# A fused adaLN attention and grouped feed-forward kernel: the first microseconds and the step places laid out anew, and the group scalars spread by DMA from a scratch row in DRAM

## The reference, cut to what matters

```python
x = x + attn(wkv(x, f, f, w1, u1, cond), Wq, Wk, Wv, Wo)      # B, T, C = 4, 256, 256
x = x + ffn(wkv(x, f, f, w2, u2, cond), ...)

def wkv(r, k, v, w, u, time_emb):
    tf = sigmoid(time_emb.sum(-1))
    decay = exp(-exp(w)) * (0.5 + 0.5 * tf)                   # per batch and channel
    ek = exp(min(k, 30)); ekv = ek * v
    # scan forward and backward over time: a = a * decay + ekv, b = b * decay + ek
    euk = exp(min(u + k, 30))
    num = nf + nb - ekv + euk * v;  den = df + db - ek + euk
    return sigmoid(r) * (num / max(den, 1e-8)) * (0.8 + 0.2 * tf)

def ffn(x):                                                   # G = 8 groups of I = 176 rows
    scores = softmax(x @ gate_w.T)                            # top 8 of E = 64 kept: w_e
    flat = w_e[:, inv_map]; scalar = flat.sum(-1)             # scalar: tokens x G
    soft = softmax(where(flat == 0, -1e9, flat))
    xg = x[:, None] + einsum('ngi,ghi->ngh', soft, mask_up_w)
    a = silu(xg @ gate_proj) * (xg @ up_proj)                 # tokens x G x 176
    return einsum('ng,ngh->nh', scalar, a @ down_proj)
```

## Time and profile before

| | us |
|---|---|
| median of 3 runs | 440.38 |
| the three runs | 440.99, 437.19, 440.38 |
| the profiled execution, its own time | 440.88 |
| its span in the trace | 438.8 |
| PE / DVE / ACT / POOL busy in it | 377.0 / 328.7 / 278.4 / 215.2 |

### The profile page before, as it was taken

The page is one execution under the profiler, slowest core; times in us unless marked ns, Lnnn a source line. Parts: engine busy times, 40 slices in busy tenths (PEclk is TensorE's granted clock), DMA queues, the critical chain, the costliest instruction groups (busy, mean ns, idle before and its releaser), DMA issues.

```text
span 438.8 us, 6479 instructions
## 1 busy us (share of the span) xinstructions
PE 377.0 (86%) x1974; PEld 301.9 (69%) x1974; DVE 328.7 (75%) x786; ACT 278.4 (63%) x675; POOL 215.2 (49%) x236
## 2 busy tenths in 40 slices
PE   0096867799998779988899898999899999999996
PEld 0086645587787568776768786787587887888884
DVE  7999568998898997479998889584666768544433
ACT  5444868699789568776879886777275243544321
POOL 4771520549354844513257202418069566786732
PEclk9998999999999998999999899999999999999999
DMA  6913410111111110200112100003023222233001
GB/s 196 323 33 118 133 40 0 49 49 51 48 49 49 49 48 3 93 3 1 48 34 61 70 0 1 24 15 108 1 73 82 98 74 58 84 95 112 25 0 48
DMA packets 11072, 26.83 MB, mean 61 GB/s; under 512 B 1312, under 2 KB 3872, under 8 KB 11040
## 3 DMA queue, kind: packets, MB, share of 16 engines
q1 hardware_dynamic: 11040, 26.44, 19.0%
HBM read 25.39 MB, written 1.05 MB: 60 GB/s over the span
## 4 chain that ended last, share of the span: by engine, by line
PE 51%; DVE 28%; ACT 11%; issue 5%; POOL 3%; DMA 1%; POOLq 0%; ACTq 0%; DVEq 0%
PE acc L1102 5%; PE acc L1104 5%; PE acc L1103 5%; PE ov L1195 4%; PE tr L1124 4%; DVE PR L1038 3%; DVE B L845 3%; PE sc L1173 3%; DVE F L845 3%; PE proj L1102 3%; PE proj L1104 2%; PE proj L1103 2%; PE tr L1104 2%; PE tr L1102 2%; PE sc L1102 2%
## 5 line engine op out<-in xcount | busy, mean ns | idle before, releaser
L568 POOL TENSOR_TENSOR WL<-stage,WH 128x256 fp32r<-128x256 f32 x146 | 120.0, 851 | 110.8 <-ACT WH L638 110.7
L588 POOL TENSOR_TENSOR PR<-PR,RI 128x512 f32<-128x512 f32 x48 | 53.5, 1129 | 85.5 <-DVE RI L1048 85.5
L1102 PE MATMUL proj<-WH,RH 128*128 128x512 f32 x96 | 42.8, 446 | 37.7 <-DVE RL L896 22.5
L1102 PE MATMUL acc<-OH,WH 128*128 128x256 f32 (+1 forms) x172 | 55.3, 321 | 5.0 <-DVE OL L1060 4.3
L601 ACT ACTIVATE PR<-PR,MX 128x128 f32<-128x128 f32 (+1 forms) x128 | 56.6, 455 | 0.5 <-DVE MX L1038 0.5
L1173 PEld LDWEIGHTS sc<-kT,QT 128*128 128x128 f32 x256 | 40.7, 191 | 19.4 <-issue 14.2
L1104 PE MATMUL acc<-OH,WL 128*128 128x256 f32 (+1 forms) x172 | 53.9, 313 | 0.0
L1103 PE MATMUL acc<-OL,WH 128*128 128x256 f32 (+1 forms) x172 | 53.9, 313 | 0.0
L1173 PE MATMUL sc<-kT,QT 128*128 128x128 f32 (+1 forms) x256 | 47.7, 328 | 3.2 <-DVE MX L1038 3.2
L1102 PEld LDWEIGHTS proj<-WH,RH 128*128 128x128 f32 x96 | 18.6, 194 | 45.1 <-issue 40.7
L1195 PE MATMUL ov<-PTS,V 128*128 128x512 f32 x96 | 46.9, 597 | 1.4 <-DVE OL L1060 1.4
(11 more groups left out here) (166 smaller groups left out, 894.9 us busy)
## 6 DMA issues: line engine op xcount, KB each, us to landing
stage<-in_ffn SPq DMA_DIRECT2D x22, 384.0 KB, 3.1
stage<-in_wq SPq DMA_DIRECT2D x8, 512.0 KB, 3.5
stage<-in_wo SPq DMA_DIRECT2D x8, 512.0 KB, 3.5
PR<-in_tables SPq DMA_DIRECT2D x4, 352.0 KB, 7.4
fT<-in_fT SPq DMA_DIRECT2D x4, 256.0 KB, 4.1
xT<-in_xT SPq DMA_DIRECT2D x4, 256.0 KB, 4.5
stage<-in_wk SPq DMA_DIRECT2D x2, 512.0 KB, 4.8
stage<-in_wv SPq DMA_DIRECT2D x2, 512.0 KB, 3.3
```

Source lines behind the costliest of these rows:

```text
L568: i = pool.tensor_tensor(lo[:, c:c + 256], src[:, c:c + 256], hi[:, c:c + 256].bitcast(F32), ALU.subtract)
L588: pool.tensor_tensor(pr, pr, RI[:, m % 4, hs[0]:hs[0] + nh].rearrange("p (h o) -> p h o", o=1).broadcast_to([P, nh, 512 // nh]), ALU.mult) ...
L1102: mm(o, lh, rh, start=first, stop=False, skip_group_check=True)
```

## The change

It has four parts.

1. **Start.** `cond` and `vecs` are loaded from ACT's queue, not SP's. The table `decay` is gone: ACT makes `DEC` from `half` with `edec` as its scale, and `half_mix` and `qks` are made later, inside the first scan call. `EX` is cleared half by DVE ahead of the first reduction and half by POOL right behind its first memset, where POOL cleared all of it behind the first split. The low part of the first key weights, `WL` of ("split", "K", 0), is made by DVE in one operation of 1024 columns, where POOL made it in four.
2. **Projections.** `project` issues the four products with the high part of the weights first and waits for the low part only before the last two.
3. **Places.** `ORDERS`, `START` and the lists of places are changed: among others K1 (0, 2) and the rest of scan call (1, 1) stand earlier, the scores' maximum (C) stands at the end of a place on DVE and not near the start of the next, the key and value steps of pair 1 stand elsewhere, the "ind" steps are gone.
4. **Group scalars.** `GS`, `IND`, `SCX` and the DVE part of route 8 are gone. Route 8 leaves 8 rows of 512 scalars in `SCR`; SP writes them to DRAM, waits, and reads each row back, repeated over the partitions that belong to its group, into one of three buffers `SBC`. The last operation of GU reads `SBC` in SBUF and not the bank `ov`.

```diff
 START = {
-    "PE": [("split", "K", 0), ("small",), ("split", "Q", 0), ("K1", 0, 0), ("R", 0), ("R", 1), ("R", 2),
-           ("K1", 0, 1), ("R", 3), ("R", 4), ("R", 5), ("K3", 0, 0), ("K3", 0, 1)],
+    "PE": [("split", "K", 0), ("small",), ("split", "Q", 0), ("K1", 0, 0), ("R", 0), ("K1", 0, 1), ("R", 1),
+           ("R", 2), ("R", 3), ("R", 4), ("R", 5), ("K3", 0, 0), ("K3", 0, 1)],
...
-    "PE": ["GA", "GB", "GS", "Y", "last", "split"],
-    "ACT": ["GT", "last", "split", "GH"],
+    "PE": ["GA", "GB", "Y", "last", "split"],
+    "ACT": ["GT", "split", "last", "GH"],
...
-    for half, places in (((0, 1), [4, 4, 4, 5, 5]), ((1, 0), [15, 15, 15, 16, 16]), ((1, 1), [19, 20, 20, 21, 21])):
+    for half, places in (((0, 1), [2, 4, 4, 5, 5]), ((1, 0), [15, 15, 15, 16, 17]), ((1, 1), [17, 18, 18, 19, 19])):
...
+            def spread_scalars(f):
+                p, m = divmod(f, FT)
+                if m == 0:
+                    tok = slice(p * PT_, (p + 1) * PT_)
+                    sp.wait_ge(s["rt_act"], 7 * p + 7)
+                    sp.dma_start(group_scalars[:, tok], SCR[:, tok]).then_inc(s["scalars_out"], 16)
+                    sp.wait_ge(s["scalars_out"], 16 * (p + 1))
+                if f >= NBC:
+                    sp.wait_ge(s["a_ready"], f - NBC + 1)
+                for g, lo, hi in group_rows(m):
+                    sp.dma_start(SBC[lo:hi, f % NBC, :], group_scalars[g, p * PT_:(p + 1) * PT_].partition_broadcast(hi - lo)).then_inc(spread_in[f % NBC], 16)
+
             for n in range(6, len(BLOCKS)):
+                if BLOCKS[n][0:2] == ("split", "F") and BLOCKS[n][2] >= 4:
+                    spread_scalars(BLOCKS[n][2] - 4)
                 load(n)
...
+            act.dma_start(cond[:], ins["cond"]).then_inc(s["cond_in"], 16)
+            act.dma_start(vecs[:], ins["vecs"]).then_inc(s["vecs_in"], 16)
...
-                            i = nc.scalar.activation(DEC[:, TE * ch:TE * ch + T], const[:, 0:T], ACT.Identity, scale=0.0,
-                                                     bias=decay[:, L - 1, ch, b:b + 1])
+                            i = nc.scalar.activation(DEC[:, TE * ch:TE * ch + T], half[:, b:b + 1].broadcast_to([P, T]), ACT.Copy,
+                                                     scale=edec[:, 4 * (L - 1) + ch:4 * (L - 1) + ch + 1])
...
-                wait_split(pe, wst)
+                pe.wait_ge(s["split_hi"], SPLIT_NO[wst] + 1)
...
                 for ch in range(CH):
-                    a = [x[:, p, ch, P * t:P * t + P] for x in (RH, RL)]
-                    w = wblock(wst, 512 * ch, 512 * ch + 512)
-                    i = three(proj[:], a[0], a[1], w[0], w[1], ch == 0, ch == CH - 1)
+                    mm(proj[:], rh[ch], wh[ch], start=ch == 0, stop=False, skip_group_check=True)
+                    mm(proj[:], rl[ch], wh[ch], start=False, stop=False, skip_group_check=True)
+                wait_split(pe, wst)
+                for ch in range(CH):
+                    i = mm(proj[:], rh[ch], wl[ch], start=False, stop=ch == CH - 1, skip_group_check=True)
...
-                    dve.wait_ge(s["scal_full"], f + 1)
+                    dve.wait_ge(spread_in[f % NBC], 16 * spread_count(f))
```

More of the change, by code:

```diff
@@ L27 @@
 BIG = 3.0e38
[L28 removed]
+NSTAGE, NSLOT, NPS, NBC = 3, 6, 4, 3
 KCAP = 30.0
@@ L91 @@
-            ("K2", 0, 0), ("wkv", 1, 1, 6)],
-    "POOL": [("split", "K", 0), ("small",), ("clear",)],
+            ("wkv", 1, 1, 0), ("split", "K", 0), ("wkv", 1, 1, 2), ("wkv", 1, 1, 3), ("wkv", 1, 1, 4), ("K1", 0, 0), ("K1", 0, 1),
+            ("wkv", 1, 1, 5), ("K2", 0, 0), ("wkv", 1, 1, 6)],
+    "POOL": [("split", "K", 0), ("small",)],
 }
 RELEVANT = {
-    "PE": {"R": None, "split": None, "small": None, "ind": None, "K1": None, "V": None, "K3": None, "GA": None, "GB": None,
-           "GS": None, "route": (0, 1, 3, 4, 6, 7, 8)},
@@ L98 @@
[L98 removed]
+    "PE": {"R": None, "split": None, "small": None, "K1": None, "V": None, "K3": None, "GA": None, "GB": None,
+           "route": (0, 1, 3, 4, 6, 7, 8)},
+    "ACT": {"split": None, "small": None, "K1": None, "V": None, "K2": None, "K3": None, "table": None,
             "wkv": (1, 6, 7), "gate": (0, 1), "route": (0, 2, 3, 5, 6, 7, 8)},
     "DVE": {"K1": None, "K2": None, "table": None, "onehot": None, "wkv": (0, 2, 3, 4, 5, 6, 8), "gate": (0, 1),
[L101 removed]
+            "route": (1, 2, 4, 5, 6, 7)},
@@ L153, in make_plan @@
     ahead = []
-    for f, places in enumerate(([36, 37, 38], [45, 45, 45])):
-        for kind, i in zip(("GA", "GB", "GS"), places):
+    for f, places in enumerate(([36, 37, 37], [45, 45, 45])):
+        for kind, i in zip(("GA", "GB"), places):
             if i < END:
@@ L218 @@
 PLAN = PLANS["PE"]
-BLOCKS = [s for s in PLAN if s[0] in ("small", "split", "ind") or s[0] == "R" and s[1] >= 6]
+BLOCKS = [s for s in PLAN if s[0] in ("small", "split") or s[0] == "R" and s[1] >= 6]
 BLOCK_NO = {s: n for n, s in enumerate(BLOCKS)}
@@ L307, with group_rows, spread_count, program @@
         unit_tr[units_before(_m) + _j] = TR[("D", _m, _j)]
-def program(nc, ins, out):
+def group_rows(m):
+    first, last = P * m // FI, (P * m + P - 1) // FI
+    return [(g, max(g * FI - P * m, 0), min((g + 1) * FI - P * m, P)) for g in range(first, last + 1)]
+def spread_count(f):
+    return sum(len(group_rows(k % FT)) for k in range(f % NBC, f + 1, NBC))
+def program(nc, ins, out, group_scalars):
     ctx = ExitStack()
@@ L422, in program @@
         staged = [sem(f"staged{k}") for k in range(NSTAGE)]
+        spread_in = [sem(f"spread_in{k}") for k in range(NBC)]
         block = ctx.enter_context(nc.Block())
@@ L549, in _ @@
             linked(pool.memset(V[:], 0.0))
+            for a in range(2):
+                i = pool.memset(EX[:, 1, a, :].bitcast(F32), 0.0)
+            i.then_inc(s["tables_cleared"], 1)
             pool.wait_ge(s["mup_in"], 16)
@@ L814, in _ @@
             v.memset(DEC[:], 0.0).then_inc(s["pads_ready"], 1)
+            for a in range(2):
+                i = v.memset(EX[:, 0, a, :].bitcast(F32), 0.0)
+            i.then_inc(s["tables_cleared"], 1)
+            dve.wait_ge(s["cond_in"], 16)
+            v.tensor_reduce(tf[:, 0:B], cond[:], X, ALU.add).then_inc(s["init_dve"], 1)
             dve.wait_ge(s["pads_ready"], 2)
@@ L1353 @@
     out = nc.dram_tensor("out_0", (P, CH, B * T), F32, kind="ExternalOutput").ap()
-    program(nc, ins, out)
+    scalars = nc.dram_tensor("group_scalars", (G, B * T), F32, kind="Internal").ap()
+    program(nc, ins, out, scalars)
     r = run_bass_kernel_spmd(nc, [arrays], core_ids=[0])
```

156 lines of the change are left out of this document (61 added, 95 removed), and 5 rows, old and new, of the table ORDERS.

## The result

| | before | after |
|---|---|---|
| median, us | 440.04 (437.19 to 440.99, 4 runs) | **419.26** (418.53 to 420.23, 4 runs) |
| profiled execution, its own time / span | 440.88 / 438.8 | 419.07 / 417.3 |
| its mean granted clock | 0.988 | 0.996 |

The ratio is 0.9537 with an interval of 0.9502 to 0.9573: 20.8 us faster, where 10.0 was forecast (430.4 us).

What follows compares the result with a forecast made beforehand. It took DVE's scan chain to bound the start, handovers attention, and PE the feed-forward part. Terms -3.5, -1.7, 0 and -4.8 gave -10.0 from 440.88, or 430.4 us on the median's scale; range 425 to 437.

Steps and rivals of the forecast that it cites:

- The other moved steps have no row ... I take 0 for all of these: Attention's unpriced moved steps: taken as 0, with 3.8 us put on both sides of the range.
- The one hole that was priced: DVE's single wait for ACT's copies of the second half of EX: worth 0 to -3.8 us, taken as 0.
- mostly the old one: Attention's order: C ending a DVE place is nearly what C near the next one's start was; taken as 0.
- Start, -3.5: Start, up to the first turned keys: initialisation and POOL out of DVE's way, 38.3 to about 35 us.
- The four contended operations and the 2.31 us one: Start, DVE beside POOL: four operations from about 1.14 to 0.62 us, -2.0; L852 from 2.31 to 0.4, -1.9.
- The low bound of -4.9: Start: the gain if no DVE operation collides with POOL, -4.9 us; the other bound was -1.
- The start carried through, not absorbed: Attention passes the start's gain on; the rival, start absorbed, gave 434 us, chance 0.13.
- High part first, -1.7: Projections: four products run before PE's wait for POOL's low parts, 1.7 us in all; 0 to -1.7 us.
- Group scalars on PE, -4.8: Feed-forward tiles: GS matmul of 0.23 us gone, 21 counted, -4.8 us; tile from 4.86 to 4.63 us.
- Group scalars on DVE, 0: Product with both operands in SBUF: at 1.14 us, +0.5 us a tile, below DVE's idle 1.6; nothing.
- The DMA's side, 0: Scalars' write and read-back: DVE about 1 and 2.5 us late, nothing lost; bounds 0 to +4 us, taken as 0.
- The price that the prediction put on it: DVE's product waiting for a whole POOL operation: 22 x 1.29 = 28 us of DVE time, judged hidden by idle rows.

Runs made afterwards that it cites:

- the third part of the lists: Changed kernel with gate and routing places, places of the first feed-forward weights, and feed-forward order of routing and split steps as before: 422.31 us, ratio 0.9643.

## Why the prediction was wrong

It was wrong in one step: **"The other moved steps have no row ... I take 0 for all of these"**. The places are worth 13.6 us with the rest of the change in place. By undoing single parts, in medians and then at equal clock: early places 4.3 and 4.4, pair 1's places 3.2 and 3.4, `ORDERS` 4.7 and 3.7, the rest 3.0 and 2.7. Their sum is 15.2 and 14.2, against 13.6 and 12.8 for all at once, so they overlap little (by the ratios the sum is 20.2 against 13.5; that much is not settled). The one hole that was priced, 3.8, was taken at 0 too, because a hole in DVE "helps only if DVE is what is late there"; with the early places undone it is back at 3.8 and the end comes 4 us later, which speaks for DVE having been late there. The sentence that attention's order "is mostly the old one" was wrong where it counted: DVE's list alone costs 4.6 (3.9 in the marks), as much as the largest hole that I had priced. In it C moved from behind the key steps that a place may hold to ahead of them, and a scan piece moved in between the norm's steps. And I had bounded all unpriced moves by the largest priced hole, 3.8. A single hole doesn't bound a sum of many short ones: from 140 to 240 us DVE waited for ACT's squares and norms ten times, 2.5 us at most, but 11.1 in all.

The other steps:

- **Start, -3.5:** -4.5 at the first turned keys; at the end 5.8 by medians, 2.6 at equal clock. The four contended operations and the 2.31 us one went as told (0.69, 0.42). The two memsets cost nothing (the reduction began at 4.01). The low bound of -4.9 was near; what was left of the collision (three scans at 1.7 us for 1.2) was as told.
- **The start carried through, not absorbed:** right in the main. The start and the early places, undone, shift all of attention by a constant in their traces, and the kernel without the new places keeps -4.9 us of output copy 0 as -4.1 at copy 31 (up to 1.7 us of both is a fall of the clock that the kernel before has more).
- **High part first, -1.7:** measured 0. I had put the whole of PE's wait for POOL on the path without asking who waits for that projection. The kernel without the edit has such waits and takes the same time.
- **Group scalars on PE, -4.8:** right. The tile is 4.63 us, the feed-forward part 4.4 shorter, the median 6.0. What the prediction missed is a coupling that goes with it: `GS` of a tile waited for DVE's last operation in the tile ahead, so that with the new routing order PE waited 1.9 us and the clock fell. With `GS` that order costs 3.6 to 4.2 us; without it, it costs nothing (in the third part of the lists, the old order even made the feed-forward part 1.0 us longer).
- **Group scalars on DVE, 0:** right. The product took 0.97 us in the mean and up to 1.26, where 1.14 was taken; its 6.3 us more lie in idle time, which fell from 33.3 to 25.1 us.
- **The DMA's side, 0:** right. DVE waited 1.3 and 1.6 us, for 1 and 2.5 forecast, and PE not at all. The 8.5 us were called the slowest load with the engines full; they are a median of two loads, and the DMA share of that stretch is 0.76.

Beside the places, part of the gain is the clock's. Runs of the kernel before with a mean granted clock of 0.996 took 434.8 and 436.8 us; the profiled one, at 0.988, took 440.9. At 0.996, as in the profile after, it is therefore about 436 against 419: some 4 of the 20.8 us may be stretches at lower clock that the kernel after has less of (an estimate from these runs). Whether the change brings this about, or whether it is chance over four runs, these runs don't settle: of the kernels close to after, one profiled run shows more falls (0.986 in the mean), others as few (0.995 for DVE's old list and for pair 1's old places).

Of the rule that was weighed in the prediction (the Trainium skill, "SBUF — State Buffer", section "Who interferes with whom"): that the product would run into POOL's work in many tiles came true, and scans too ran at 1.7 us for 1.2. The price that the prediction put on it, a whole POOL operation each time, did not: what was added is at most 0.57 us (1.26 for 0.69), not the 1.29 of an `OL`. That is no fault of the rule: by that section the later one is blocked until the first has ended, which is the rest of a POOL operation and not the whole of it. The trace agrees: here are POOL's piece and DVE's product, and a product with no POOL operation beside it:

```profile
326.44 0.73 POOL L596 TENSOR_TENSOR WL<-stage,WH 128x256 fp32r<-128x256 f32 x1
326.66 1.05 DVE L1108 SCALAR_TENSOR_TENSOR PR<-PR,SBC 128x512 f32<-128x512 f32 x1
...
400.05 0.69 DVE L1108 SCALAR_TENSOR_TENSOR PR<-PR,SBC 128x512 f32<-128x512 f32 x1
```

POOL's piece had 0.51 us to go when the product was started, and the product took 0.36 more. At 321.44 it had 0.56 to go and 0.42 was added; at 371.83, 0.67 and 0.54; at 317.15, behind an `OL` that had run for 0.93 us, 0.36 and 0.22. The added time is what is left of the POOL operation, less 0.13 to 0.15 us. Of the 22 products 16 were met in this way; the most that a piece of a split added is 0.57.

It is not always the first end that lets DVE in. In the kernel before, L852 (single input, started at 22.29) ran beside the gate split, which ended at 22.95, and ended only at 24.59, behind two of POOL's four clears; the second of these began at 23.57 and took 0.73. So the prediction's 2.31 us hold three POOL operations, not the clears alone.

## What to carry to other kernels

Where several in-order engines hand work to one another and none is full, look at the order inside the stage before its totals: sum all short waits of the engine that others wait for, and use that sum, not the largest wait, to judge what a new order may bring. Here DVE's waits for ACT in attention were 38.4 us, the new order took 12.3 of them away, and attention became 13.0 shorter. That the two go together is what one case shows, not a rule. When a move puts independent work into a round trip between engines, or brings forward what another engine waits for, price it at that round trip in every place where it recurs. And test an order together with the edits that come with it: a part of an order may cost 4 us until a coupling of buffers (here bank `ov`) has gone.

## What the runs showed of the hardware that was not expected

The granted clock of TensorE falls between its two levels (2.4 and 1.2 GHz) for short stretches, at places that change from one kernel to the next though the instructions there are the same. Up to output copy 10 the kernel with the third part of the lists undone keeps the marks of the kernel after. Here is its window of 144 to 160 us, then that of after:

```profile
144.00:152.00 8.00, 6.22 (x46) 5.33 (x45) 7.67 (x25) 6.63 (x19) 2.04 (x4) 0.97 0.21 66
152.00:160.00 8.00, 8.00 (x32) 5.90 (x31) 7.90 (x15) 6.95 (x17) 6.65 (x7) 0.82 0.18 63
```

```profile
144.00:152.00 8.00, 6.19 (x47) 5.26 (x46) 7.66 (x25) 6.77 (x20) 2.02 (x4) 1.00 0.20 66
152.00:160.00 8.00, 7.38 (x36) 5.40 (x34) 7.90 (x17) 7.65 (x20) 7.73 (x9) 1.00 0.19 61
```

PE had been busy 6.2 of 8 us in both; one falls and the other doesn't, and the marks behind it differ by 1.7 us. The falls shown here came in or after stretches in which PE had had gaps, though not every such stretch is followed by one. In the kernel with the extra memset the gaps are from 56 us on (PE busy 4.24 us of 8) and the fall is in the next stretch:

```profile
56.00:64.00 8.00, 4.24 (x22) 3.42 (x22) 6.70 (x25) 6.29 (x18) 2.04 (x2) 1.00 0.00 0
64.00:72.00 8.00, 6.50 (x21) 4.98 (x20) 5.89 (x14) 4.96 (x12) 1.12 (x2) 0.57 0.00 0
```

A stretch of 8 us at 0.79 holds 8 x 0.21 = 1.7 us less of PE's full-speed time, one at 0.57 holds 3.4 less. Against the kernel after, whose own fall at 56 us holds 1.7, the marks of the second moved by 2.2. Before a difference of 2 us between two kernels is explained by an edit, the clock of every stretch has to be compared.

The low parts that DVE makes (1024 columns in 1.22 us) are also cheaper than POOL's: four pieces of 256 columns took 4.31 us there, beside DVE, and one piece alone takes 0.74 in the feed-forward tiles.
